# A decoder block with routed experts: 12 of the 79 expert tiles run between the routing steps of the last sequence

## The reference

```
x = x + attn(layernorm(x))    # random-feature causal attention, 4 heads, then layernorm, W1, relu, W2
x = x + cross(layernorm(x), ctx)   # softmax attention of each sequence on its own ctx
x = x + ffn(layernorm(x)):
    logits = xf @ Wg.T                      # 16 experts
    topw, topi = top_k(softmax(logits), 2)  # normalised to sum 1 -> gates
    for e in range(16):
        h = silu(xf @ W1[e]) * (xf @ W3[e])     # 176 wide
        out = out + gates[:, e:e+1] * (h @ W2[e])
```

## Time and profile before

| | us |
|---|---|
| median of 3 runs (lowest, highest) | 822.21 (821.16, 823.55) |
| the profiled execution, its own time | 823.12 |
| its span, first to last instruction | 821.3 |
| busy in it: PE, DVE, ACT, POOL | 798.6, 598.0, 432.8, 396.8 |

### The profile page before, as it was taken

How to read it: one execution, slowest core, us unless ns; L and a number is a source line. 1 busy time by engine, 2 the same in 40 slices (tenths; PEclk the granted TensorE clock), 3 DMA queues, 4 the chain that set the end, 5 groups by cost and what they waited for, 6 DMA issues and landing times.

```text
span 821.3 us, 21021 instructions
## 1 busy us (share of the span) xinstructions
PE 798.6 (97%) x5949; PEld 758.3 (92%) x5950; DVE 598.0 (73%) x1722; ACT 432.8 (53%) x1185; POOL 396.8 (48%) x567
## 2 busy tenths in 40 slices
PE   9999999999999999999999999999988999999995
PEld 8898999999999999999999999999987799999994
DVE  4757777888787877878787778887675566666663
ACT  4473554637265463737355453726243267667673
POOL 3332134444534454454535444353435358787875
PEclk9999999999999999999999999999999999999997
DMA  8786573655739284564828375573499458777780
GB/s 266 256 290 233 194 256 120 244 204 193 256 125 308 81 281 161 201 242 160 280 95 309 108 254 175 187 263 127 156 425 368 146 106 134 127 132 128 131 132 2
DMA packets 105673, 161.19 MB, mean 196 GB/s; under 512 B 10672, under 2 KB 69616, under 8 KB 104752
## 3 DMA queue, kind: packets, MB, share of 16 engines
q1 hardware_dynamic: 79264, 115.33, 42.0%
q0 software_dynamic: 15792, 35.17, 17.2%
q10 hardware_dynamic: 10576, 10.19, 4.7%
HBM read 50.14 MB, written 112.47 MB: 198 GB/s over the span
## 4 chain that ended last, share of the span: by engine, by line
PE 82%; DVE 6%; ACT 6%; issue 3%; DMA 1%; SPq 1%; POOL 1%; POOLq 0%; DVEq 0%; ACTq 0%
PE ps L797 70%; PE ps L808 5%; PE ps L1037 3%; PE ps L1147 2%; PE ps L1169 2%; ACT fT_hi L1305 2%; ACT relu_v L1306 2%; ACT phi L1292 1%; DVE fT_lo L1508 1%; DVE snmax L1681 1%; DVE smax L1677 1%; DVE pr L1670 1%; DVE xn_attn L1501 0%; ACT pr L1351 0%; DVE stat L1490 0%
## 5 line engine op out<-in xcount | busy, mean ns | idle before, releaser
L788 POOL DMA_INDIRECT out<-narrow,sidx x79 | 122.4, 1549 | 46.1 <-DVE sidx L1886 20.7
L1220 ACT ACTIVATE xn3T<-ps 128x512 f32<-128x512 f32 x17 | 10.2, 597 | 138.8 <-PE ps L808 136.2
L797 PE MATMUL ps<-w_hi,fT_hi 128*128 128x256 f32 x256 | 79.8, 312 | 2.4 <-DVE fT_lo L1508 2.1
L1292 ACT ACTIVATE phi<-ps,nmax 128x128 f32<-128x128 f32 x256 | 73.4, 381 | 9.2 <-DVE nmax L1629 9.0
L1508 DVE TENSOR_TENSOR fT_lo<-relu_v,fT_hi 128x512 fp32r<-128x512 f32 x64 | 52.3, 818 | 33.2 <-ACT relu_v L1306 33.0
L797 PE MATMUL ps<-w_lo,fT_hi 128*128 128x256 f32 x256 | 72.3, 282 | 0.0
L797 PE MATMUL ps<-w_hi,fT_lo 128*128 128x256 f32 x256 | 72.2, 282 | 0.0
L1306 ACT ACTIVATE relu_v<-ps,b_sb 128x256 f32<-128x256 f32 x128 | 69.1, 540 | 0.0
L1305 ACT ACTIVATE fT_hi<-ps,b_sb 128x256 fp32r<-128x256 f32 x128 | 68.0, 531 | 1.5 <-PE ps L797 1.5
L605 POOL TENSOR_TENSOR veps<-mv,eps_ln 128x2 f32<-128x2 f32 x48 | 10.8, 225 | 118.4 <-DVE mv L1494 118.4
L797 PE MATMUL ps<-hT_hi,w_hi 128*128 128x256 f32 x256 | 67.2, 284 | 0.0
(11 more groups left out here) (300 smaller groups left out, 2744.6 us busy)
## 6 DMA issues: line engine op xcount, KB each, us to landing
expert_rows<-zero_rows SPq DMA_DIRECT2D x16, 4352.0 KB, 16.0
narrow<-expert_rows ACTq DMA_DIRECT2D x71, 136.0 KB
expert_up_hi<-X SPq DMA_DIRECT2D x16, 352.0 KB, 2.7
e_lo<-expert_up_lo POOLq DMA_DIRECT2D x2, 2816.0 KB, 12.8
e_hi<-expert_up_hi POOLq DMA_DIRECT2D x2, 2816.0 KB, 22.1
part_raw<-in_E SPq DMA_DIRECT2D x30, 176.0 KB
expert_up_lo<-part_raw SPq DMA_DIRECT2D x15, 352.0 KB, 3.1
X<-in_x SPq DMA_DIRECT2D x16, 256.0 KB
```

What stands on the lines that cost most here:

```text
L788: pool.indirect_dma_start(out_rows, bass.IndirectOffsetOnAxis(sidx[:, u:u + 1], 0), yg[:, u, :], None, bounds_check=NT * P - 1, oob_is_err ...
L797: return pe.matmul(out_, lhsT, rhs, start=start, stop=stop)
L1220: return act.activation(out_, in_, ACT.Copy)
L1292: last = act.activation(phi[:, g, h, :], ps[:, g, h * M:(h + 1) * M], ACT.Exp, bias=nmax[:, g, h:h + 1])
```

## The change

Twelve tiles (`EARLY`) are planned from the counts of the first 13 sequences (`EARLY_SEQS`): only tiles that these fill whole, floor(count / 128) per expert, in the order of experts (`early_count`, `early_sum`, `early_tiles`, in turn 16 on DVE). Turn 18 goes. The routing of sequence 15 is spread over the first slots of the tile stage: the router's transposes after slot 0, its product in slot 1, `choose` in 1, `gates` in 2, `place_own` in 3, the plan of the remaining tiles in 4 to 6, the edge rows in 10 to 12. The remaining 67 tiles (`taken` says how many each expert has had) follow the early ones. 24 tiles are written out where 8 were, and the loop runs three times.

Among early tiles a different expert alone makes tile s wait for s - 1 and s - 2 (`early_waits`); for tiles 12 and 13 the meeting with early ones is forced to 1. SP, not ACT, loads the rows of tiles 0 to 7 (early in turn 17) and 12 to 18 (from slot 3 on, between its waits for scatters). The exponential of the last gap is e to the power of the gap, on POOL, behind the scatter of tile 0. POOL scatters the rows of sequence 15 behind the scatter of tile 1 and gathers the edge rows behind that of tile 2. The weights are loaded by SP (the last piece by ACT) in pieces: the low upper parts of 14 experts in turn 15, the rest over turn 16. The filler matmuls after the last cross-attention and in the plan go.

```diff
+    EARLY = 12
+    EARLY_SEQS = NSEQ - 3
+    UNROLLED = 3 * GB
@@ SP, turn
+                if last_attn:
+                    hold(sp, x2_stored, 16 * (NSEQ - 4))
+                    load_up_lo(0, 0, KEPT_LAST)
                 for p in splits:
                     keep_part(p)
+                if last_attn:
+                    sp.wait_ge(proj_ps, NSEQ * 4)
+                    load_up_lo(1, 0, KEPT_LAST)
+                if last_ffn:
+                    sp.wait_ge(wo_ps, NSEQ)
+                    load_weights(e13_hi[:, 0], up_hi_dram[:, 0], em_loaded)
+                    for c in range(DC):
+                        load_up_lo(c, KEPT_LAST, NE)
+                    sp.wait_ge(w1_ps, NSEQ * 4)
+                    load_weights(e13_hi[:, 1], up_hi_dram[:, 1], em_loaded)
+                    sp.wait_ge(w2_ps, NSEQ)
+                    load_weights(e2a[0], down_hi_dram, e2_loaded)
+                    load_weights(e2b[0:LO + IR], rest_dram, e2_loaded)
+                if last_cross:
+                    load_early()
@@ SP
+            def load_early():
+                sp.wait_ge(early_plan, EARLY_TILES)
+                sp.wait_ge(zeroed, 16 * (NSEQ + 1))
+                sp.wait_ge(placed, EARLY_SEQS * 16 * TOPK * TS)
+                tiles = [tile_of(s) for s in range(3)]
+                sp.wait_ge(snmax_ready, NSEQ)
+                for s in range(GB):
+                    load_tile(s, tiles[s] if s < len(tiles) else tile_of(s))
+            def load_late(s):
+                if s == EARLY:
+                    sp.wait_ge(plan_ready, 1)
+                tile = tile_of(s)
+                if s == EARLY:
+                    sp.wait_ge(placed, NSEQ * 16 * TOPK * TS)
+                hold(sp, sidx_ready, s - (GB - 1))
+                hold(sp, yg_ready, s - (GB - 1))
+                load_tile(s, tile)
...
             def slot_tiles(s, u, last):
-                if isinstance(s, int) and s == 1:
+                if isinstance(s, int) and LATE_FROM <= s < LATE_FROM + GB - 1:
+                    load_late(EARLY + s - LATE_FROM)
+                if isinstance(s, int) and s == EARLY:
                     sp.wait_ge(ranges_ready, 1)
...
+            sp.wait_ge(early_plan, EARLY_WAITS)
             in_groups(slot_tiles, sp)
@@ POOL
-            pool.wait_ge(row_ready, 2)
-            pool.wait_ge(placed, NSEQ * 16 * TOPK * TS)
+            def choice_odds():
+                pool.wait_ge(gap_ready, NSEQ)
+                pool.tensor_tensor(egap[:, :], euler[:, :], gap[:, :], ALU.pow).then_inc(egap_ready, 1)
...
+            def slot_tiles(s, u, last):
+                scatter(s, u)
+                if first(s):
+                    choice_odds()
+                if isinstance(s, int) and s == 1:
+                    store_rows(NSEQ - 1)
+                if isinstance(s, int) and s == 2:
+                    gather_edges()
@@ PE
-            keep_clock(2, 9)
...
-            keep_clock(2, 10)
             turn_rows(0, 0)
             turn_rows(1, 1)
+            pe.wait_ge(em_loaded, 16 * 6)
             up(0, 0)
...
+                if first(s):
+                    last_router_rows()
+                if isinstance(s, int) and s == 1:
+                    router(NSEQ - 1, 4)
+                if isinstance(s, int) and s == 3:
+                    count_choices(NSEQ - 1, 4)
+                if isinstance(s, int) and s == 6:
+                    late_numbers()
+                if isinstance(s, int) and s == EARLY - 2:
+                    edge_rows()
@@ DVE
+            def early_count():
+                dve.wait_ge(place_ready, EARLY_SEQS)
+                dve.tensor_tensor(total[:, :], carry[:, 0, :], place0[:, :], ALU.subtract).then_inc(early_plan, 1)
+                dve.wait_ge(early_plan, EARLY_COUNTED)
+                then(dve.tensor_copy(need_i[:, :], total[:, :]))
+                then(dve.tensor_scalar(need_s[:, :], need_i[:, :], 7, None, ALU.logical_shift_right))
+                then(dve.tensor_copy(need[:, :], need_s[:, :]))
+            def early_waits():
+                dve.wait_ge(early_plan, EARLY_TILES)
+                for k in range(1, ADDING):
+                    last = dve.tensor_tensor(other_early[:, k - 1, k:], expert_i[:, k:EARLY], expert_i[:, 0:EARLY - k],
+                                             ALU.not_equal)
+                then(last)
+                for k in range(1, ADDING):
+                    last = dve.scalar_tensor_tensor(added_need[:, k - 1, k:EARLY], other_early[:, k - 1, k:], 16.0,
+                                                    round_of[:, 0:EARLY - k], ALU.mult, ALU.add)
+                last.then_inc(early_plan, 1)
@@ DVE, meeting_tiles
+                for k in range(1, ADDING):
+                    last = dve.tensor_scalar(meeting[:, k - 1, EARLY:EARLY + k], meeting[:, k - 1, EARLY:EARLY + k], 1.0, None,
+                                             ALU.max)
+                then(last)
@@ DVE, slot_tiles
+                if isinstance(s, int) and s == 1:
+                    logits_in(NSEQ - 1, 4)
+                    hold(dve, logit_ready, NSEQ)
+                    choose(NSEQ - 1)
+                    choice_seen(NSEQ - 1)
+                    early_waits()
+                if isinstance(s, int) and s == 2:
+                    dve.wait_ge(egap_ready, NSEQ)
+                    gates(NSEQ - 1)
+                if isinstance(s, int) and s == 3:
+                    place_own(NSEQ - 1, 4)
+                if isinstance(s, int) and s == 4:
+                    late_count()
+                if isinstance(s, int) and s == 5:
+                    late_sum()
+                if isinstance(s, int) and s == 6:
+                    late_tiles()
```

More of the change, by code:

```diff
@@ L367, in in_turns @@
             turn(NSEQ + 1, None, None, NSEQ - 1, NSEQ - 2, None)
-            turn(NSEQ + 2, None, None, None, NSEQ - 1, None)
         def in_groups(step, eng, begin=None):
-            for u in range(GB):
-                step(u, u, False)
-            with eng.Fori(0, (SLOT_TILES // GB - 2) // 2) as g:
+            for s in range(UNROLLED):
+                step(s, s % GB, False)
+            with eng.Fori(0, (SURE - UNROLLED) // (2 * GB)) as g:
                 if begin is not None:
@@ L597, in _ @@
             pool.wait_ge(const_ready, N_CONST - 2)
-            for whole, short in ((before, before_01), (ones, ones_01)):
-                pool.tensor_copy(short[:, :], whole[:, :]).then_inc(const_ready, 1)
+            for whole, short in ((before, before_01), (ones[:, :], ones_01)):
+                pool.tensor_copy(short[:, :], whole).then_inc(const_ready, 1)
             pool.wait_ge(const_ready, N_CONST)
@@ L720, in turn @@
                         split_ctx(b + 1)
-                if r is not None and not last_turn:
+                if r is not None:
                     keep_rows(r)
@@ L1461, in slot_tiles @@
                     rows_hi(s + 2, (u + 2) % GB)
-                if not (first(s) or last):
+                fetches = not (first(s) or last or (isinstance(s, int) and EARLY <= s + GB - 1 < EARLY + GB - 1))
+                if fetches:
                     tile = tile_of(s + (GB - 1))
@@ L1468, in slot_tiles @@
                 hidden_hi(s, u)
-                if not (first(s) or last):
+                if fetches:
                     load_rows(s + GB - 1, (u - 1) % GB, tile)
+                if first(s):
+                    act.wait_ge(logit_ps, NSEQ - 1)
+                    copy_router_rows(NSEQ - 1, ps[:, 6:8, 0:S])
+                    own_rows(rows_last)
             in_groups(slot_tiles, act)
@@ L1613, in logits_in, with choice_seen, summed @@
                     .then_inc(logit_ready, 1)
+            def choice_seen(r):
+                hold(dve, chosen, (r + 1) * CHOICE_STEPS)
+                dve.tensor_tensor(oh[:, :, :], hot[:, 0], hot[:, 1], ALU.add).then_inc(oh_ready, 1)
+                if not first(r):
+                    dve.wait_ge(egap_ready, r)
+                dve.tensor_tensor(gap[:, :], best[:, :, 1], best[:, :, 0], ALU.subtract)\
+                    .then_inc(gap_ready, 1)
+            def summed(counted):
+                cum, cbufs, n = counted, (cum_a, cum_b), 1
+                while n < NE:
+                    dst = cbufs[0]
+                    cbufs = cbufs[::-1]
+                    dve.tensor_copy(dst[:, 0:n], cum[:, 0:n])
+                    then(dve.tensor_tensor(dst[:, n:], cum[:, n:], cum[:, 0:NE - n], ALU.add))
+                    cum, n = dst, 2 * n
+                return cum
@@ L1758, in turn @@
                 if last_cross:
[L1759 removed]
+                    dve.wait_ge(egap_ready, r + 1)
+                    gates(r)
                 if nxt is not None:
@@ L1767, in turn @@
                         part_rest(p, n)
-                if b is not None:
+                if b is not None and not last_cross:
                     if not first(b):
@@ L1788, in turn @@
                     first_sum(f)
```

(2 more changed lines are left out.)

356 lines of the change are left out of this document (199 added, 157 removed).

## The result

The changed kernel took 843.9 us (median of 4 runs, 842.96 to 844.97), the kernel before 822.09 (4 runs, 821.16 to 823.55): ratio 1.0264, 95% interval 1.0244 to 1.0284. It is slower, as forecast, and 7.9 above the forecast of 836, 0.9 above the upper end of the range. The profiled execution took 842.96 for a span of 841.2, which is 19.9 more than before; the forecast had 13.9 more.

A forecast was written before the change was run, and what follows sets the result against it. PE, busy 97%, was taken to bound the kernel before; after the change POOL ends last: S(0) 639.4 plus 81.7 gives S(21) 721.1, S(78) 828.3, plus 6.9 the end 835.2. Forecast 836 us, range 827 to 843.

The forecast's parts named there:

- T(0): T(s): start of tile s's hidden transposes on PE, tiles from 0; tile 0 at 631.8 us, 18.9 earlier than before.
- S(0): S(s): start of tile s's scatter on POOL; the first at 639.4 us, bounds 638.4 and 641.4, waiting for the early waits.
- twelve waited steps: Scatters in the first 22 tiles awaiting the landing of the one just before: 12 x 5.0 = 60.0 us.
- eight free steps: Scatters of tiles 4, 6, 8, 9, 10, 14, 17, 20, following without a landing wait: 1.85 us each, 14.8 together.
- S(21): Scatter of tile 21 on POOL at 721.1 us (718.0 to 724.6), where it was 703.64.
- T(31): Hidden transposes of tile 31 on PE, held by the eight buffers: 726.9 us, before 715.0.
- The buffer rule: With eight buffers, PE starts tile s no sooner than 5.8 us after the scatter of tile s - 10 starts.
- Weights: Weight loads ahead of the tiles: down weights in at 620.5 us or some later, used about 633; delay 0, bounds 0 and +3.
- Start of the tiles: Rows for tiles 0 to 7, asked for early, land in 2.1 us, before PE finishes the attention at 626.6.
- the second rival: POOL's scatters land in 2.7 us instead of 3.8, a wait costs 3.9 instead of 5.0, end 822, no change; chance 0.05.
- The first (the waits don't decide): Landing waits of POOL's scatters don't decide, the early start comes through: 811 us; holds from four waits down; chance 0.12.
- The third (the clock): PE's clock falls between 686 and 727, some three tiles behind 727 run slow: T(76) 824.5, time 840 us; chance 0.15.

The follow-up runs named there:

- experiments 1 and 2: Scatters go to four scratch copies, no waits for earlier neighbours, experts' sum left out: 1 in the changed kernel, 817.12 us; 2 in the kernel before, 824.52.
- experiment 9: Changed kernel without loading the lower half of the first down weights (2048 KB); its product reads the upper half, output numbers differ: 839.68 us, ratio 1.0208.
- Experiments 5 and 9: 5: changed kernel, last piece of the lower down weights asked for by SP behind the row loads, not by ACT ahead: 843.8 us. For 9 see its line.
- Experiment 7: Changed kernel with SP's row loads of tiles 12 to 18 put behind its leave for the slot's scatter: 843.88 us, ratio 1.0257.
- Experiment 6: Changed kernel with the early waits written by DVE in slot 0, ahead of the last sequence's choice: 839.85 us, ratio 1.0205.
- experiments 5 to 10: Edits of the changed kernel; 8 joins those of 5, 6 and 7: 844.97 us; 10 joins those of 9 and 6: 834.74 us.
- experiment 3: Changed kernel, complete, with experts taken 14 down to 0, then 15 (the turned order): 834.14 us, ratio 1.0119, span 829.9.

## Why the prediction was right in direction and 6 us short

Its steps, with what was measured in the profiled execution:

| step | forecast | measured |
|---|---|---|
| T(0) | 631.8 | 635.72 |
| T(7) | 654.1 | 656.37 |
| S(0) | 639.4 (to 641.4) | 643.06 |
| twelve waited steps, sum | 60.0 | 57.7 |
| S(2) - S(1), row stores | 6.9 | 7.03 |
| eight free steps, sum | 14.8 | 17.9 |
| S(21) | 721.1 (718.0 to 724.6) | 725.61 |
| T(31) | 726.9 | 731.18 |
| S(21) to S(78) | 107.2 | 109.4 |
| from S(78) to the end | 6.9 | 6.2 |

The misses sum to the difference: +3.7 at S(0), +0.8 from there to S(21) (3.1 less 2.3), +2.2 behind it, -0.7 at the end: 6.0, which is 841.2 less 835.2. The median of the runs lies 0.9 above the profiled execution, and that put it outside the range.

**The mechanism held.** The waits are where they were forecast to be, at 4.81 us on the mean against 5.0, and experiments 1 and 2 take them away: 28 us. The buffer rule held too. T(s) >= S(s - 10) + 5.8 gives, within 0.5, 698.8, 703.4, 709.9 and 714.6 for tiles 22, 23, 25 and 26 with the measured S; their transposes start at 698.31, 703.08, 710.01 and 714.70. T(31) is 5.6 behind S(21).

**The step that failed stands under *Weights*: "Cover: 10 us. ... I take 0, bounds 0 and +3"**, and with it the 2.1 us for the landing of rows under *Start of the tiles*. The row behind that 2.1 was read at 645 us, where the DMA engines had been nearly idle (share 0.04 from 644 to 646); the load was moved to 620, into weights. And the end of the weights was reckoned at 620.5 at 432 GB/s, "some us later". The three sets of down weights landed at 615.5, 623.5 and 628.9. Two things go with that: they are not asked for before 606.8, when the dense layer has ended, so that the engines moved only 241 GB/s from 604 to 608; and from 616 to 620 the engines were full at 255 GB/s, with routing's row stores and a store of `out` among the weights. Which of these slowed them was not isolated; experiment 9, without the last set, has 254 there too. These are the changed kernel's stretches:

```profile
604.00:608.00 4.00, 4.00 (x36) 3.96 (x36) 3.63 (x14) 0.22 (x1) 0.00 (x0) 1.00 0.66 241
...
616.00:620.00 4.00, 4.00 (x26) 3.71 (x26) 2.56 (x9) 1.31 (x3) 2.73 (x3) 1.00 0.99 255
```

The trace of the kernel before could have told it. Its DMA engines are as full, in a stretch on which the forecast is silent (columns as above; a packet counts where it starts, so a share can pass 1):

```profile
620.00:624.00 4.00, 3.86 (x22) 3.18 (x22) 2.10 (x12) 1.58 (x5) 3.08 (x4) 1.00 1.07 417
624.00:628.00 4.00, 4.00 (x27) 3.68 (x26) 2.69 (x11) 0.24 (x2) 1.11 (x4) 1.00 2.04 276
628.00:632.00 4.00, 2.82 (x15) 1.86 (x13) 2.29 (x12) 0.43 (x1) 2.10 (x3) 1.00 1.00 299
```

Nobody waited for them there, since T(0) was at 650.65. Experiments 5 and 9 show it: with the same bytes in another order the wait moves from the rows to the weights (4.6 to 5.0), with 2 MB less it is gone, and T(0) is at 631.29, 0.5 from the forecast. The sign that the forecast had set itself for this, PE idle for rows or weights before 650, came true. The step is worth 3.7 of the 6.0.

**Terms that were mis-sized.** The free steps beside SP's row loads, 2.62 instead of 1.85 for tiles 4, 6, 8 and 9, 3.1 in all: I had followed the late loads as rows for PE, and not as instructions that SP runs between two leaves. Experiment 7 shows that the 0.8 goes where the load goes. The first scatter's 3.7 is no term of its own: from T(0) to S(0) it took 7.34, where 7.6 was forecast, so all of it is T(0)'s lateness. Experiment 9, which mends T(0), gives 4.3 back at S(0). Experiment 6 shows only that the order of DVE's work ahead of S(0), which the forecast had read rightly, could be better by 2.2. Behind tile 21: tile 45's step was 4.39 where 3.37 was taken, tile 26's 2.69 where 1.85 was, and 0.35 and 0.19 at tiles 56 and 63. Of this 1.0 to 1.7 us belong to the one execution profiled: in the six other kernels with this order and all waits (experiments 5 to 10) tile 45's step is 3.61 to 4.07, tile 26's at most 2.08 and S(78) - S(21) 107.7 to 108.4. (The forecast's words count 22 and 33 steps from S(22) to S(78), one too few; its 828.3 holds all 56.) The waits erred to the other side by 2.3, of which 1.3 is tile 18 alone (see the second rival).

**The rivals.** The first (the waits don't decide) fell with experiment 1. It had said of itself that it holds from four waits down; the turned order has four and gave 829.9, not 811, since the small steps of POOL's chain, summed up under experiment 3, were missing in it.

The second (landings at the short end, 3.9 per wait) came true for one of twelve, tile 18 with 3.73. It was never open to the others., titled all scatters, has its landings from the ten of 79 that the trace shows, and its 2.7 is of tile 74, one of the empty slots behind the 71 real tiles. This is the same view of the kernel before for the scatters from 806 to 808:

```profile
DMA to landing us min/median/max: 2.7/2.7/2.7
```

Tile 18 waits for tile 17, which by the counts in the forecast holds a single row of expert 3 (385 = 3 x 128 + 1); in all seven kernels with this order and all waits its step is 3.72 to 3.85.

The third (the clock): it did fall, to 0.59 and 0.56 in the stretches 628 to 636 and to 0.88 from 692 to 735, part of the time at 1.2 GHz after PE had stood, and was back at 1.00 from 735 on. Between 692 and 735 it fell three times, to 0.72, 0.57 and 0.78 over 4 us, behind 4 us in which PE had worked 1.6, 1.9 and 3.2. The second of them:

```profile
710.00:714.00 4.00, 1.88 (x14) 1.58 (x13) 1.20 (x6) 0.90 (x3) 1.90 (x2) 1.00 0.34 47
714.00:718.00 4.00, 4.00 (x21) 4.00 (x21) 1.38 (x6) 2.07 (x6) 1.54 (x1) 0.57 0.50 103
```

T(76) was 824.89, where that rival had 824.5, but that is luck: T(31) was 4.3 late because S(21) was 4.5 late, and from there to T(76) it took 93.7, where the kernel before took 92.0, so the clock behind T(31) cost at most 1.7 of the rival's 5.6. And the end was POOL's: S(76) came 6.4 behind T(76), and the rival had 3.5. Whether the low clock cost the end anything was not isolated.

## What to carry to other kernels

When work is moved earlier, read every transfer that it needs in the stretch where it will now run, not where it ran before; DMA engines that are full while nobody waits for them hide a bound until someone comes earlier. If the bytes are the bound, putting one transfer ahead of another only renames the wait. And count a chain of scatters that must wait for each other by their landing, not their issue: a neighbour that must be awaited cost 2.6 times a free one here (4.81 and 1.85), and the order in which tiles of different experts follow each other decided 11 us.

## What the runs showed of the hardware that I had not expected

- A row load of 136 KB landed in 2.1 us where the DMA engines had been nearly idle, in 3.0 with the last set of weights left out and in 3.8 with it asked for later (one load each), and the first in 9.64 behind two sets of down weights (3.9 MB) that were asked for before it and landed at 623.5 and 628.9.
- Full DMA engines (share 0.99 to 1.07) moved between 255 GB/s (616 to 620) and 434 (600 to 604).
- A scatter of a full tile landed in 3.5 to 4.5 us in nearly all cases seen, one of an empty slot in 2.7, and one of a single row let its waiting neighbour follow after 3.73.
- Reading a number into a register on SP took two steps of 0.27 and 0.15 us in the chain of waits, and a row load with its tile number lengthened the time between two leaves by 0.8.
- Taking the experts in another order alone costs the kernel before 0.5% (828.63 against 824.09), by landing waits at later tiles (5.04 at tile 64).
